# Half of each layer norm moved ahead of the stage barrier in a fused two-layer perceiver on one core

## The reference, cut to what matters

```python
x = x + L0_xattn(layernorm(x), ctx)   # cross attention over frequencies
x = x + L0_attn(layernorm(x))         # gated attention, then x1 + mlp(layernorm(x1))
x = x + L0_ffn(layernorm(x))          # gated mlp and routed experts
x = x + L1_xattn(layernorm(x), ctx)   # attention over ctx and own tokens
x = x + L1_attn(layernorm(x))         # a state space recurrence
x = x + L1_ffn(layernorm(x))          # ternary mlp with a low-rank path
```

## Time and profile before

| | |
|---|---|
| Median of 3 runs | 2288.76 us |
| Lowest and highest | 2284.0 and 2290.79 us |
| The profiled execution | 2282.55 us |
| Its span, first to last instruction | 2280.8 us |
| TensorE busy | 2114.9 us, 93% |
| VectorE busy | 1250.1 us, 55% |
| ScalarE busy | 917.8 us, 40% |
| Mean granted TensorE clock | 0.972 |

### The profile page before, as it was taken

The page is one execution under the profiler, slowest core; times in us unless marked ns, Lnnn a source line. Parts: engine busy times, 40 slices in busy tenths (PEclk is TensorE's granted clock), DMA queues, the critical chain, the costliest instruction groups (busy, mean ns, idle before and its releaser), DMA issues. The chain is left out here.

```text
span 2280.8 us, 35869 instructions
## 1 busy us (share of the span) xinstructions
PE 2114.9 (93%) x14950; PEld 1537.2 (67%) x14950; DVE 1250.1 (55%) x2086; ACT 917.8 (40%) x2208; POOL 91.5 (4%) x119
## 2 busy tenths in 40 slices
PE   6989898789999999989998999999999999988899
PEld 5764444468867787844445788778878777764587
DVE  4246466363344888799998310544353443537563
ACT  3224343143424333499996432332232322213342
POOL 0000001000000000100000000000000000000122
PEclk9999898799999999999999999999999999989999
DMA  6120000111210110120003044321121211232000
GB/s 236 39 80 1 1 2 2 39 56 38 74 43 19 38 56 19 56 93 19 1 1 111 27 159 148 98 80 48 43 84 43 84 43 43 66 112 91 1 1 37
DMA packets 84872, 127.01 MB, mean 56 GB/s; under 512 B 6998, under 2 KB 48470, under 8 KB 84248
## 3 DMA queue, kind: packets, MB, share of 16 engines
q1 hardware_dynamic: 84712, 124.73, 16.6%
HBM read 109.77 MB, written 14.94 MB: 55 GB/s over the span
## 5 line engine op out<-in xcount | busy, mean ns | idle before, releaser
L1170 ACT ACTIVATE R<-bank 128x512 f32<-128x512 f32 (+3 forms) x157 | 93.2, 597 | 461.9 <-PE bank L869 329.6
L1397 ACT ACTIVATE R<-R 128x64 f32<-128x64 f32 x1024 | 248.5, 373 | 0.0
L869 PE MATMUL bank<-cth,wmh 128*128 128x512 f32 x512 | 207.9, 406 | 13.4 <-ACT arena L1494 7.6
L869 PE MATMUL bank<-cth,wml 128*128 128x512 f32 x512 | 202.1, 395 | 0.0
L869 PE MATMUL bank<-ctl,wmh 128*128 128x512 f32 x512 | 201.9, 394 | 0.0
L500 PE MATMUL bank<-XN,arena 128*128 128x512 f32 x320 | 149.8, 623 | 0.5 <-ACT R L1330 0.5
L869 PEld LDWEIGHTS bank<-cth,wmh 128*128 128x128 f32 x512 | 96.1, 188 | 42.2 <-issue 23.0
L500 PE MATMUL bank<-Y,arena 128*128 128x512 f32 x256 | 116.3, 599 | 0.0
L500 PEld LDWEIGHTS bank<-XN,arena 128*128 128x128 f32 x320 | 62.7, 201 | 76.6 <-issue 75.6
L2123 DVE COPY Y<-bank 128x512 f32<-128x512 f32 x128 | 79.3, 681 | 59.5 <-PE bank L907 59.4
L869 PEld LDWEIGHTS bank<-cth,wml 128*128 128x128 f32 x512 | 96.1, 188 | 22.2
(11 more groups left out here) (413 smaller groups left out, 4439.5 us busy)
## 6 DMA issues: line engine op xcount, KB each, us to landing
H<-in_ctxT SPq DMA_DIRECT2D x30, 512.0 KB, 5.1
arena<-in_L_attn_mlp_w SPq DMA_DIRECT2D x8, 1024.0 KB, 5.3
arena<-spill SPq DMA_DIRECT2D x32, 256.0 KB, 5.5
spill<-R SPq DMA_DIRECT2D x3, 2048.0 KB, 8.3
spill<-XN SPq DMA_DIRECT2D x3, 2048.0 KB, 8.3
arena<-in_L_ffn_Wg SPq DMA_DIRECT2D x4, 1024.0 KB, 7.4
arena<-in_L_ffn_Wu SPq DMA_DIRECT2D x4, 1024.0 KB, 5.3
arena<-in_L_ffn_Wd SPq DMA_DIRECT2D x4, 1024.0 KB, 5.5
```

Source lines behind the costliest of these rows:

```text
L869: last = mm(b[:, :].rearrange("p (a c) -> p a c", a=2), w_, c_[:, k, :, :], start=(k == 0 and n_ == 0), stop=(k == 3 and n_ == 2))
L1170: fn(dst, src, ACT.Copy).then_inc(act_bank_free, 1)
L1397: last = fn(EE[n % 3][:, a:a + 64], RC["Ey"][:, t, h, :], ACT.Copy, scale=RC["Ex"][:, t, h, 8 * j + x:8 * j + x + 1])
```

## The change

Half 0 (tiles 0 to 3) of each norm, that is `token_rows(l, 0)`, its statistics, roots, `standardise`, `features(l, 0)` and ScalarE's copies, moves ahead of the barrier, into the stage that produces the stream. Its rows go into four of ScalarE's banks (`row_bank` finds them for VectorE, which now counts `act_bank_free` for them). Half 1 stays behind the barrier in VectorE's banks.

- The last products of stages 2 and 6 are ordered so that half 0 of the stream is complete first. In stages 1, 2, 3 and 6 the rows go in after the sixth (stage 6: seventh) of eight products, VectorE's `standardise` before its add of the last, and `features(l, 0)` after the last product.
- In stage 4 the rows stand before the last two `factors_out`, in stage 5 before the last pair's `prob_tail`, with `features(4, 0)` before `out_rows(15)`; VectorE does the statistics and `standardise(4, 0)` before the last pair's `weighted`.
- ScalarE's `inputs(0)` of norms 1 and 5 and the split `cth` of stage 5 move ahead of the barrier too; `inputs_low(0)` moves ahead at norm 5 only. In stage 5, `memory(0, range(7))` is no longer interrupted.
- `z` of some norms lies elsewhere, for buffers free on both sides of the barrier (`halves`, `one`).
- SyncE issues the clock weights before the first barrier's wait, and `load_ct(1, ct)` waits for the fourth barrier instead of for `cth`.

```diff
             def token_rows(l, c):
                 for t in range(4 * c, 4 * c + 4):
-                    b = open_dve(("lt", l, t))
+                    b = open_dve(("lt", l, t)) if c else open_act(("lt", l, t))
...
-                    last.then_inc(dve_bank_full, 1)
+                    last.then_inc(dve_bank_full if c else act_bank_full, 1)
...
                           (lambda k: first_low[:, 3, k, tl(o)], lambda k: lk_low[:, k, ch(c)])).then_inc(dve_bank_full, 1)
+                    if (o, c) == (1, 1):
+                        on_dve(("ao", 3, 0))
+                        token_rows(0, 0)
             free_after_dve("ao")
+            features(0, 0)
             end_stage()
...
-            for o in range(4):
-                for c in range(C2):
+            for c in range(C2):
+                for o in range(4):
                     b = open_dve(("bo", o, c))
...
+                    if (o, c) == (1, 1):
+                        on_dve(("bo", 3, 0))
+                        token_rows(1, 0)
             free_after_dve("bo")
-            end_stage()
-            token_rows(1, 0)
+            features(1, 0)
+            end_stage()
             token_rows(1, 1)
-            features(1, 0)
...
+            on_dve(("cf", 3, 3))
+            token_rows(3, 0)
             factors_out(STEPS - 2)
             factors_out(STEPS - 1)
+            features(3, 0)
             end_stage()
...
-            token_rows(3, 0)
+            token_rows(3, 1)
             pe.wait_ge(S["d_wlo"], 2)
-            memory(0, range(2))
-            token_rows(3, 1)
-            memory(0, range(2, 5))
-            features(3, 0)
-            memory(0, range(5, 7))
+            memory(0, range(7))
             features(3, 1)
...
                 fill(5)
+                if pr == PAIRS - 1:
+                    token_rows(4, 0)
                 prob_tail(pr)
                 fill(6, 7)
                 weighted(b0)
                 weighted(b1)
+            features(4, 0)
             out_rows(PAIRS - 1)
...
+            for oc in ((2, 0), (3, 0), (2, 1), (3, 1)):
+                ed_then(ed_first(*oc), *oc)
+                if oc == (2, 1):
+                    on_dve(("ed", 3, 0))
+                    token_rows(5, 0)
+            features(5, 0)
+            end_stage()
```

On ScalarE (stage 4's end), VectorE (stages 1, 3, 4 and 5) and SyncE:

```diff
+            warm()
+            deviations(3, 0)
+            features(3, 0)
+            act.wait_ge(S["d_ct"], 32)
+            fn(cth[:, :, :, :], ct_first, ACT.Copy).then_inc(S["d_chi"], 1)
             end_stage()
...
+                    if (o, c) == (3, 1):
+                        standardise(0, 0)
                     add_to_stream(("ao", o, c), o, c, col("L0_xattn_bo", o))
+                    if (o, c) == (1, 1):
+                        statistics(0, 0)
             end_stage()
...
+                        if then is not None and (o, c) == (3, 1):
+                            standardise(then, 0)
                         add_to_stream((name, j, c, o), o, c, col(bias, o) if j == 0 else None)
                         if c == C2 - 1:
                             split_low(piece_no[((name, j), o)] + PIECES)
+                            if then is not None and o == 1:
+                                statistics(then, 0)
...
             memory_low(0)
+            statistics(3, 0)
+            memory_low(1)
             from_factors(STEPS - 2)
-            memory_low(1)
+            standardise(3, 0)
             from_factors(STEPS - 1)
             end_stage()
...
+                elif pr == PAIRS - 1:
+                    statistics(4, 0)
+                    standardise(4, 0)
                 on_act(("sc", b1, 3))
...
-            sp.wait_ge(S["d_chi"], 1)
+            sp.wait_ge(stage_done, 4 * 4)
             load_ct(1, ct)
```

More of the change, by code:

```diff
@@ L601, in _ @@
             for c in range(C2):
-                features(0, c)
+                if c:
+                    features(0, c)
                 normed(pe, 0, c)
@@ L750, in split_linear, with down @@
                 return last
-            def down(name, j, ready, first):
+            def down(name, j, ready, first, then=None):
                 for c in range(C2):
@@ L771, in _ @@
                         features(1, 1)
-                down("b2", j, S["h_low"], 0)
+                down("b2", j, S["h_low"], 0, 2 if j == NQ - 1 else None)
+            features(2, 0)
             end_stage()
-            token_rows(2, 0)
             token_rows(2, 1)
@@ L779, in _ @@
             for c in range(C2):
-                features(2, c)
+                if c:
+                    features(2, c)
                 normed(pe, 2, c)
@@ L1054, in _ @@
             for c in range(C2):
-                features(4, c)
+                if c:
+                    features(4, c)
                 normed(pe, 4, c)
@@ L1251, in _ @@
                        ).then_inc(S["a_ahi"], 1)
+            warm()
+            deviations(0, 0)
+            features(0, 0)
             end_stage()
@@ L1501, in out_rows @@
                          b[:, :].rearrange("p (i o q) -> p i o q", i=2, o=8))
-            warm()
-            split_high(0)
-            for c in range(C2):
-                deviations(3, c)
+            deviations(3, 1)
+            fn(dx_high[:, :, ch(0)], XN[:, :, ch(0)], ACT.Copy).then_inc(S["d_xhi"], 1)
             for n in range(4):
                 d_piece_high(n)
-            memory(0, (0, 1, 4))
-            for c, more in ((0, (5, 6)), (1, (7,))):
+            memory(0, (0, 1, 4, 5, 6))
+            for c, more in ((1, (7,)),):
                 features(3, c)
@@ L1551, in _ @@
                        ).then_inc(S["f_abs"], 1)
+            warm()
+            deviations(4, 0)
+            features(4, 0)
             out_rows(PAIRS - 1)
@@ L1590, in inputs @@
                     fn(Yh[:, k, ch(c)], unit(("feat", 5, c, k))[:, :], ACT.Copy).then_inc(S["f_yhi"], 1)
-            def low_rank_mix(c):
-                fn(Z2[:, ch(c)], unit(("z2", c))[0:LR, :], ACT.Copy, scale=col("gate", 0, LR)).then_inc(S["f_zhi"], 1)
             warm()
@@ L1597, in _, with low_rank_mix @@
             inputs(0)
+            end_stage()
+            def low_rank_mix(c):
+                fn(Z2[:, ch(c)], unit(("z2", c))[0:LR, :], ACT.Copy, scale=col("gate", 0, LR)).then_inc(S["f_zhi"], 1)
             deviations(5, 1)
@@ L1649, in stored, with row_bank @@
                 dve.wait_ge(dve_bank_free, UV.at[key] + 1)
+            def row_bank(l, t):
+                if t >= 4:
+                    return unit(("lt", l, t))
+                u = UA.at[("lt", l, t)]
+                dve.wait_ge(act_bank_full, u + 1)
+                return UA.banks[u % 4]
             def statistics(l, c):
@@ L1654, in statistics @@
                 for t in tiles:
-                    last = v.bn_stats(NS["st"][:, t, :], unit(("lt", l, t))[:, :])
+                    last = v.bn_stats(NS["st"][:, t, :], row_bank(l, t)[:, :])
                 step(last)
@@ L1670, in standardise, with second_half @@
                 for t in range(4 * c, 4 * c + 4):
-                    v.tensor_scalar(spec["z"][:, t, :], UV.banks[UV.at[("lt", l, t)] % 4][:, :], NS["mv"][:, t, 0:1],
-                                    NS["std"][:, 0, t:t + 1], ALU.subtract, ALU.mult).then_inc(dve_bank_free, 1)
-            def layernorm(l):
-                for c in range(C2):
-                    statistics(l, c)
-                    standardise(l, c)
+                    v.tensor_scalar(spec["z"](t), row_bank(l, t)[:, :], NS["mv"][:, t, 0:1],
+                                    NS["std"][:, 0, t:t + 1], ALU.subtract, ALU.mult).then_inc(dve_bank_free if c else act_bank_free, 1)
+            def second_half(l):
+                statistics(l, 1)
+                standardise(l, 1)
             def add_to_stream(key, o, c, bias=None):
@@ L1877, in _ @@
                     spread_norm(o + 1)
-            for o in range(4):
-                for c in range(C2):
+            for c in range(C2):
+                for o in range(4):
+                    if (o, c) == (3, 1):
+                        standardise(1, 0)
                     b = unit(("bo", o, c))
@@ L1888, in inputs_low @@
                 last.then_inc(S["x_low"], 1)
-            statistics(1, 0)
-            standardise(1, 0)
-            statistics(1, 1)
+            inputs_low(0)
             split_low(0)
             split_low(1)
-            inputs_low(0)
-            standardise(1, 1)
+            second_half(1)
             step(v.tensor_tensor(XT[:, :, 0:512], XT[:, :, 0:512], Y[:, :, 0:512], ALU.add))
```

136 lines of the change are left out of this document (70 added, 66 removed).

## The result

The changed kernel is faster. Beside the kernel before on the same chip it took 2262.44 us (median of 4; 2261.87 to 2268.11) against 2286.38 (median of 4; 2283.18 to 2290.79): a ratio of 0.991, 95% interval 0.9892 to 0.9927, which is a gain of 20.6 us (16.7 to 24.7). The forecast gain was 17.3. A gain in us is throughout (1 - ratio) times the median of before, so it can differ from the difference of the two medians, here 23.9. The profiled execution of the changed kernel is the slowest of its four, 2268.11 us, and that of the kernel before, 2282.55, is faster than the four above, so this pair of traces shows less than the medians: a span of 2266.3 against 2280.8, 14.5 less.

The account below looks back on a forecast made before the run. TensorE, busy 2114.9 of 2280.8 us, was taken as the bound. The terms, 5.1 + 0.9 + 5.3 - 2.4 + 4.9 + 3.5 = 17.3 us, take the median from 2288.76 to 2271.5 us, range 2263 to 2284.

Parts of the forecast that it names:

- norms 0 and 2: First and third stage ends: `clock` and `cq` start earlier, right behind the second-half rows; gains 5.1 and 5.3 us.
- the 3 us that would have refuted it: Forecast is wrong if features 0 wait more than 3 us for VectorE at norms 0, 2 or 5.
- The first rival: Standardise and copies ahead of the barrier are exposed at five ends: 10 us go, gain 7, time 2281.5; chance 0.14.
- the second: Nothing happens: waits only move, at all six ends; gain 0 to 5, time 2287; chance 0.10 (nothing within 0.3%).
- Norm 1: Second stage end: most of 4 us earned returns as a wait for VectorE; gain 0.9, range 0 to 1.9.
- Norm 3: Fourth stage end: loaded VectorE queue and `cth` split delay the barrier to 1254.2; loss 2.4 us, bounds 0.6 and 4.
- Norm 4: Fifth stage end: 6.4 us gained behind the barrier less 1.5 for `output`; gain 4.9, bounds 2 and 6.4.
- it ends 1.5 later: At norm 4, `output` starts 2.9 us later, loses half of its 2.9 us low clock, so ends 1.5 later.
- Norm 5: Sixth stage end: features 1 wait for VectorE until 2137.25 against 2140.74; gain 3.5 us, bounds 2 and 4.6.
- The table loads: Behind norm 4's barrier ScalarE has three table loads of 1.28 us, now two; 2.66 us each would cost 4.1 more.
- The clock rival: Low clock would fall on products behind the barrier; at 14 us per end, time 2312; slower by clock, chance 0.04.
- The loads: Loads tied to a barrier, none used within 14 us of it: costed at nothing; without cover one is some 5 us.
- Its sign of being wrong: Forecast is wrong if an untouched stage (attention pairs, the experts) changes its length by more than 2 us.

Follow-up runs that it names:

- the second comparison: The changed kernel run again, unedited, beside the kernel before: 2265.37 us (median of 6), ratio 0.9926 (0.9903 to 0.9948).

## Why the prediction was right, and where its sizes were off

**The method held.** The bounds on the gain, 7.1 and 22.8, take in what both comparisons found. At norms 0 and 2 the forecast gave, counted from each arrival, the barrier and the next product to 0.3 us: `clock` at 155.85 against 155.56, the barrier's transposes at 153.8 against 153.66, and `cq` at 663.7 against 660.02 + 3.39 = 663.4. The waits ahead of features 0 were 1.50, 0.50, 1.82 and 1.16 at norms 0, 1, 2 and 5, under the 3 us that would have refuted it. The first rival, a barrier that takes it back at five ends, is thereby out, and so is the second, since norms 0 and 2 alone gave 11.9.

**Norm 1**: the mechanism as told, a wait for VectorE that returns the gain. Features 1 start at 476.77 + 2.96 = 479.7, forecast 479.95; then they run at the low clock, which leaves 0.4 of the gain. That was named as the risk. In two of six traces with this order they ran at full clock, and the end gained 2.0 over the trace before. The mean of 1.9 is the upper bound of the forecast, whose own start times for features 1, 481.21 and 479.95, already differ by 1.3.

**Norm 3**: the barrier came as reckoned, 1244.91 + 9.08 = 1254.0 for 1254.2. The term -2.4 was mis-sized: it measured -1.15 here and -0.7 in the means. Its own parts, 0.6, 1.3 and 1.0, add up to 2.9; the prediction gives no reason for 2.4. The low clock fell on the row transposes alone (3.53) and was over when the `memory` products started, so the 1.0 put down for those wasn't paid. One argument was wrong beside it: that a gap of 3.16 between busy stretches didn't lower the clock. The same gap did in another execution of the same order; and in two more traces the gap of 2.5 ahead of the first `memory` product did.

**Norm 4**, 4.9, is the term that was off most in the pair of traces, 7.8, and is the one where the pair misleads: the means give 4.7. The part behind the barrier was exact: from the end of `output` to `dl(1)` it was 2069.85 - 2051.07 = 18.78 and is 2057.79 - 2045.41 = 12.38, which is 6.4, and the means, 19.5 and 13.1, give 6.4 too. For the other part, "it ends 1.5 later", the pair has `output` end 1.4 earlier; but the trace before has by far the latest end of the four with the old order. Over all, it ends 1.7 later. The way to this number was wrong in two steps that cancel. `output` doesn't keep half of its low clock, but loses all of it, in eight traces of nine (14.08, where the old order has 16.3 on average); and it starts 3.6 later and not 2.9.

**Norm 5**, 3.5 against 2.4, in the pair and in the means: features 0 come where they should, but the second rows run at half rate (3.32 instead of 1.97), ahead of VectorE's statistics, so features 1 stand at 2126.27 + 12.06 = 2138.33 instead of 2137.25.

**The table loads.** Three loads of 1.28 stand behind the barrier as forecast, each operation 1.29 to 1.30 behind the start of its load. The Trainium skill, "ScalarE: Activation LUTs", section "What ACT_TABLE_LOAD costs", puts a switch at about 2.66 us, the load and a drain of about 1.4 together; the trace agrees on the load and shows no drain, and taking one load away moved `dl(1)` by 1.0.

**The clock rival.** It was half right: the clock matters, but the change takes low spells away more than it adds them. Norms 0 and 2 have none now, at norm 4 it shrinks from `output` to one group of transposes, while norms 1 and 3 got one more each. Filling the gaps and doing nothing else gained 7.1 us (4.6 to 9.6), so the clock was already a cost of the kernel before, at transposes which VectorE's chain waits for. The prediction called those spells harmless because the transposes wait anyway; at norm 0 they cost 1.5. "TensorE: Matmul & The Clock Gate" of the Trainium skill, section "HAM oscillation", says that idle gaps are paid again in what follows; the filled gap bears that out.

**The loads** were costed at nothing, and no run shows otherwise. The one candidate is the `XN` load of the first pair: it leaves 8.0 earlier with its stage (1419.06 after), but its user is only 7.0 early, in both executions of the changed kernel. The kernel with only norm 4 moved has the same wait, 4.24 us, without the change's loads of stage 5.

**Its sign of being wrong.** The prediction named as one that an untouched stage changes its length by more than 2 us. Stage 5 did, by 3.7. The sign was too narrow: in the five traces with its old order this stage differs by up to 4.1 us (729.7 and 733.8).

**What the sum owes to chance.** The terms of the six ends sum to 20.5 in the pair of traces, which is the 20.6 of the first comparison; the second comparison gave 16.9, which is the forecast's 17.3 nearly. The interval of each holds all of these. In the means the six ends sum to 18.5. That this lies 1 us from the forecast is partly luck: norm 1 gave 1.0 and norm 3 1.7 more than put down, norm 5 1.1 less. Why a spell falls into stage 2 or 5 in one execution and not in the next stays open: no run here shows it.

## What to carry to other kernels

Move the first half of a serial chain ahead of a barrier when the engine that it idles has products left that need nothing from it; count what stands ahead of it in each engine's queue, because a step that is put last before a barrier (here VectorE's low split and ScalarE's `cth`) is paid by all engines once nothing else holds the barrier: moving two such steps gained 5.5 us in its stretch, as much as norm 0 or 2. Price a wait together with the clock behind it: filling a 3.6 us gap with unused transposes gained 1.5 us at one place. And take a term of one or two microseconds from several executions, or from an experiment that undoes it, since two executions of one kernel differ by that much in a single stage: of norm 4 the one pair said 7.8, and ten traces said 4.7.

## What was not expected of the hardware

- Unused work made the kernel faster: 3 x 26 transposes, 3.0 us each group, for 7.1 us less (4.6 to 9.6).
- The same gap of 3.16 to 3.17 us ahead of the same product left the granted clock at 1.00 in one execution and was followed by 0.50 in another; the 128 x 512 products took 0.63 instead of 0.39 to 0.40 there. A shorter gap, 2.51 to 2.52 us at the start of the same stage, was followed by 0.50 in two of five traces and by 1.00 in three.
- Granted clock below 1.00 was also seen inside a pair of stage 5, at 0.72 over 6 us, in one execution and not in another of the same kernel, with 1.4 us lost at that place.
